# Attention in 64 units on one Trainium2 core: the copy of the attended values waits for earlier outputs, and the softmax's last sum and minimum become one operation per head

## What is computed

```python
x = rmsnorm(hidden_states, ln_weight)
h_q, h_k, h_v = x @ w_q.T, ctx @ w_k.T, ctx @ w_v.T          # 32 heads of 128
score = einsum('bqhd,bkhd->bhqk', h_q, h_k) + position_bias
score = where(mask, score, -inf)
attn = einsum('bhqk,bkhd->bqhd', where(mask, softmax(score), 0), h_v)
out = hidden_states + attn @ w_out.T
```

## Time and profile before

| what | value |
|---|---|
| three runs | 1131.38, 1131.36, 1126.65 us; median 1131.36 |
| the profiled execution | 1131.8 us, its span 1130.0 us |
| mean granted clock of PE in the span | 0.939 |
| busy: PE, DVE, POOL, ACT | 1042.1, 810.8, 552.7, 516.4 us |
| attention loop | some 372 to 979 us, 37.6 us for one pair of heads |

### The profile page before, as it was taken

The page is one execution under the profiler, slowest core; times in us unless marked ns, Lnnn a source line. Parts: engine busy times, 40 slices in busy tenths (PEclk is TensorE's granted clock), DMA queues, the critical chain, the costliest instruction groups (busy, mean ns, idle before and its releaser), DMA issues.

```text
span 1130.0 us, 18045 instructions
## 1 busy us (share of the span) xinstructions
PE 1042.1 (92%) x5664; PEld 902.2 (80%) x5664; DVE 810.8 (72%) x1389; ACT 516.4 (46%) x1279; POOL 552.7 (49%) x507
## 2 busy tenths in 40 slices
PE   8999999999999779888988898889888988899995
PEld 7887888999999668777877787778777877677874
DVE  6778676665655788777977797779777977854525
ACT  6744454322222545545554555455545555245251
POOL 0356665544532665454645564556555555324113
PEclk9999999999999898889988998899889988799998
DMA  7534444544442623122312231223222312110010
GB/s 253 179 127 160 159 163 173 179 157 169 150 159 94 218 75 117 60 79 93 116 60 79 93 116 61 81 90 116 63 80 89 116 42 94 51 53 1 1 38 37
DMA packets 57585, 119.81 MB, mean 106 GB/s; under 512 B 7232, under 2 KB 11328, under 8 KB 57536
## 3 DMA queue, kind: packets, MB, share of 16 engines
q1 hardware_dynamic: 57536, 119.19, 31.2%
HBM read 83.51 MB, written 35.65 MB: 105 GB/s over the span
## 4 chain that ended last, share of the span: by engine, by line
PE 69%; DVE 4%; issue 4%; ACT 3%; POOL 1%; ACTq 0%; POOLq 0%; DVEq 0%
PE psum L1772 18%; PE psum L1773 18%; PE psum L1774 18%; PE psum L1778 9%; PE psum L1779 3%; PE psum L1934 2%; DVE pt L1336 1%; ACT av_hi L924 1%; ACT mix L924 1%; ACT pt L924 1%; POOL stat L865 0%; PE psum L2029 0%; DVE rsum L1682 0%; POOL mix L694 0%; POOL stat L867 0%
## 5 line engine op out<-in xcount | busy, mean ns | idle before, releaser
L694 POOL TENSOR_TENSOR mix<-kf,mix 128x512 fp32r<-128x512 f32 x64 | 82.2, 1284 | 262.7 <-ACT mix L924 262.6
L1772 PE MATMUL psum<-mix,av_hi 128*128 128x256 f32 (+1 forms) x512 | 180.8, 353 | 3.4 <-POOL mix L694 1.9
L1778 PE MATMUL psum<-pt,av_hi 128*128 128x256 f32 x256 | 77.3, 378 | 61.6 <-DVE pt L1336 60.4
L924 ACT ACTIVATE av_hi<-psum 128x512 fp32r<-128x512 f32 x76 | 45.1, 594 | 172.1 <-PE psum L1774 126.7
L1778 PEld LDWEIGHTS psum<-pt,av_hi 128*128 128x128 f32 x256 | 57.0, 223 | 70.9 <-DVE pt L1336 67.6
L1772 PE MATMUL psum<-xn_lo,ext_hi 128*128 128x512 f32 x256 | 112.8, 441 | 0.0
L1772 PEld LDWEIGHTS psum<-mix,av_hi 128*128 128x128 f32 x512 | 98.7, 193 | 12.1 <-POOL mix L694 2.1
L1773 PE MATMUL psum<-xn_hi,ext_lo 128*128 128x512 f32 x256 | 106.8, 417 | 0.0
L1774 PE MATMUL psum<-xn_hi,ext_hi 128*128 128x512 f32 x256 | 104.9, 410 | 0.0
L1774 PE MATMUL psum<-mix,av_hi 128*128 128x512 f32 x256 | 102.5, 400 | 0.0
L1773 PE MATMUL psum<-mix,av_lo 128*128 128x512 f32 x256 | 102.0, 399 | 0.0
(11 more groups left out here) (251 smaller groups left out, 3235.4 us busy)
## 6 DMA issues: line engine op xcount, KB each, us to landing
kf<-k_blocks SPq DMA_DIRECT2D x64, 256.0 KB, 2.7
wvq_hi<-v_blocks SPq DMA_DIRECT2D x64, 256.0 KB, 2.8
raw<-in_wk SPq DMA_DIRECT2D x16, 512.0 KB, 3.6
k_blocks<-far SPq DMA_DIRECT2D x32, 256.0 KB, 2.2
raw<-in_wv SPq DMA_DIRECT2D x16, 512.0 KB, 4.3
v_blocks<-rows SPq DMA_DIRECT2D x32, 256.0 KB, 2.2
raw<-in_wq SPq DMA_DIRECT2D x16, 512.0 KB, 3.2
raw<-in_wo SPq DMA_DIRECT2D x16, 512.0 KB, 3.3
```

The costliest lines, as they stand in the source:

```text
L694: g.tensor_tensor(dst_lo, src, dst_hi, ALU.subtract).then_inc(s_lo, 1)
L924: return a.activation(dst, src, ACT.Copy)
L1772: mm(out, lhs(0), rhs(1), start=first, stop=False)
L1778: mm(out, lhs(0), rhs_both, start=True, stop=False)
```

## The change

Three things change together.

First, in attended_hi for j = 0 the count is 8g - 8 in the place of 8g - 4. The others keep theirs.

Second, the scores carry the opposite sign: the norm weights `lnw` are multiplied by -1 once on POOL, `far` holds +2^100 for a masked key, the bias is subtracted, and the exponential is taken with scale -1. The maximum becomes a minimum, clamped by starting at 2^99. Each head's last sum and its minimum are one call, tensor_tensor_reduce, which DVE carries out as two instructions. The semaphore scores_full counts four a unit, and its users' counts are multiplied by four.

Third, attended is cut in two: `rest` (attended_rest) stands between the first sum and the minimum operations.

```diff
@@ gpsimd
+                    g.tensor_scalar(lnw[:, :], lnw[:, :], -1.0, None, ALU.mult).then_inc(s_lnw_negated, 1)
+                    pool.wait_ge(s_lnw_negated, 1)
                 g.tensor_tensor(rows[:, tile % 2], rows[:, tile % 2], lnw[:, :], ALU.mult).then_inc(s_xn_ready, 1)
...
-                nc.gpsimd.tensor_tensor(bm, far[:, HB * hf:HB * hf + HB, :], g_, ALU.add).then_inc(s_bm_ready, 1)
+                nc.gpsimd.tensor_tensor(bm, far[:, HB * hf:HB * hf + HB, :], g_, ALU.subtract).then_inc(s_bm_ready, 1)
@@ scalar
-                act.wait_ge(s_max_neg, n + 1)
+                act.wait_ge(s_scores_full, 4 * n + 4)
...
-                    a.activation(soft[parity][:, b, :], soft[parity][:, b, :], ACT.Exp, bias=nmax[:, 1, b:b + 1],
+                    a.activation(soft[parity][:, b, :], soft[parity][:, b, :], ACT.Exp, bias=nmin[:, b:b + 1], scale=-1.0,
...
-                        attended_hi(n - 1, 8 * g - 4 + (4 if j == 3 else -4 if j == 0 else 0) + (0 if j else 4), prev(j))
+                        attended_hi(n - 1, 8 * g - 4 + (4 if j == 3 else -4 if j == 0 else 0), prev(j))
@@ vector, softmax_in
                 v.tensor_tensor(s, psS[:, :, 0], bm, ALU.add).then_inc(s_scores_sum, 1)
                 dve.wait_ge(s_scores_sum, n + 1)
-                v.tensor_tensor(s, psS[:, :, 1], s, ALU.add).then_inc(s_scores_full, 1)
-                dve.wait_ge(s_scores_full, n + 1)
-                v.tensor_reduce(nmax[:, 0, :], s, AX.X, ALU.max).then_inc(s_scores_max, 1)
-                dve.wait_ge(s_scores_max, n + 1)
-                v.tensor_scalar(nmax[:, 1, :], nmax[:, 0, :], -0.5 * FAR, -1.0, ALU.max, ALU.mult
-                                ).then_inc(s_max_neg, 1)
+
+            def softmax_min(n, parity):
+
+                s = soft[parity]
+                for b in range(HB):
+                    v.tensor_tensor_reduce(s[:, b, :], psS[:, b, 1], s[:, b, :], 1.0, 0.5 * FAR, ALU.add, ALU.min,
+                                           nmin[:, b:b + 1]).then_inc(s_scores_full, 1)
...
-            def attended(n, j):
+            def attended_rest(n, j):
 
                 dve.wait_ge(s_a_hi, n + 1)
                 v.tensor_tensor(rest[:, :, :], psA[:, :, 0], heads_out(0, j), ALU.subtract).then_inc(s_a_rest, 1)
+
+            def attended(n, j):
+
                 dve.wait_ge(s_a_rest, n + 1)
                 v.tensor_tensor(heads_out(1, j), psA[:, :, 1], rest[:, :, :], ALU.add).then_inc(s_a_lo, 1)
@@ vector, pair_dve
                     softmax_in(n + 1, (j + 1) % 2)
+                    if not (is_first(g) and j == 0):
+                        attended_rest(n - 1, prev(j))
+                    softmax_min(n + 1, (j + 1) % 2)
@@ tensor, scores
-                    pe.wait_ge(s_scores_full, n)
+                    pe.wait_ge(s_scores_full, 4 * n)
```

More of the change, by code:

```diff
@@ L119, in build @@
         prep = sb("prep", [P, 7, B])
-        nmax = sb("nmax", [P, 2, HB])
+        nmin = sb("nmin", [P, HB])
         esum = sb("esum", [P, 3, HB])
@@ L225, in build @@
         s_scores_full = sem("scores_full")
-        s_scores_max = sem("scores_max")
-        s_max_neg = sem("max_neg")
+        s_lnw_negated = sem("lnw_negated")
         s_exp_done = sem("exp_done")
@@ L1504, in group_dve @@
                     dve.wait_ge(s_kst[C12], 16 * PAIRS)
-                    v.tensor_scalar(far[:, :, :], m8[:, :, :], -1.0, FAR, ALU.add, ALU.mult).then_inc(s_far_ready, 1)
+                    v.tensor_scalar(far[:, :, :], m8[:, :, :], -1.0, -FAR, ALU.add, ALU.mult).then_inc(s_far_ready, 1)
                 dve.wait_ge(s_xc, q + 1)
@@ L1600, in _ @@
             softmax_in(0, 0)
+            softmax_min(0, 0)
             lo_of(s_q_hi, s_q_lo, 2, qk[1][:, 0], banks[5], qk[0][:, 0])
@@ L1630, in pair_dve @@
                     if last and j == 3:
+                        attended_rest(n - 1, j - 1)
                         attended(n - 1, j - 1)
@@ L1641, in pair_dve @@
                         y_stats(2)
+                        attended_rest(n, j)
                         attended(n, j)
@@ L1959, in outputs @@
                         pe.wait_ge(s_q_lo, units)
-                        pe.wait_ge(s_scores_full, units)
+                        pe.wait_ge(s_scores_full, 4 * units)
                         pe.wait_ge(s_o_add, 2 * (o - 2) + i + 1)
```

## The result

The changed kernel takes 1032.1 us (median of four runs, 1031.9 to 1033.0) against 1131.4 us (1126.7 to 1131.9). The ratio is 0.913, with a 95% interval of 0.911 to 0.916. The forecast was 1034.6 us.

What follows compares the result with a forecast made beforehand. PE was taken as the bound, stalled 15 times by a wait in attended_hi. 1131.8 - 94.7 (stalls) - 2.5 (first pair) = 1034.6 us, between 1028 and 1041; the range with rival 1 was 1027 to 1056.

Steps and rivals of the forecast that it cites:

- What bounds the kernel: Attention loop: PE is the bound; 15 stalls of 6.31 us come from attended_hi's wait for outputs in j = 0.
- The term: Attention loop, j = 0: asking for 8g - 8 outputs removes all 15 stalls of 6.31 us, 94.7 us.
- What is late next: Unit j = 0 with the new order: no stall takes the old one's place while m is below 2.9 us.
- The chain in j = 0: DVE operations from the scores' first sum to the probabilities' low part: done at 680.1 + m, PE wants them at 682.98.
- m, the new operations: DVE time for a unit's four sum-and-minimum pairs: 1.6 us, between 1.1 and 2.4.
- The sign given: Profile after, DVE: the new pair of instructions should show at about 0.4 us per head.
- The point at which DVE decides: Steady loop: DVE instead of PE sets the unit's time from m = 2.2 us on.
- The rival itself: DVE becomes the bound in the loop: at m = 2.4, 20 us more, 1055 us; chance 0.13.
- DVE's half gives PE nothing in the loop: Steady loop: DVE's unit falls from 7.80 to 7.2 us beside PE's 7.81, giving only room of 0.6 us.
- First and last pair: Ends of the loop: first pair gains 2.5 us, of 0 to 6; last pair 0, within 1.5.
- The extra pass on POOL: Sign of the norm weights, once, near 110 us: costs 0, at most 1.5 us if the transposes were late.
- The clock: Granted clock of 1.00 through the loop; rival that it does not hold: 0.95, 30 us, 1065 us, chance 0.04.

Runs made afterwards that it cites:

- the last experiment: Three kernels on one chip: changed kernel 1032.9 us, the new wait alone 1035.3 us, changed kernel with another POOL order ahead of the loop 1031.7 us.
- four sets: Changed kernel with the four sum-and-minimum pairs of each unit done four times on DVE, extra outputs unused: 1113.8 us.
- that kernel: Changed kernel with attended_hi in j = 0 asking for 8g - 5 outputs instead of 8g - 8: 1090.0 us, ratio 0.966.

## Why the prediction was right, step by step

- **What bounds the kernel.** Right. Each stall was idle time and a slow unit after it, both by the one number in attended_hi; the wait alone took all 15 away. The term was 94.7 us and measured 96.2, because the stalls cost 6.4 us on average and the pair whose rows were priced 6.31. Part of the good fit of the total is luck: the sum starts from an execution of 1131.8 us, at the top of what the kernel before showed. On the chip of the last experiment its median is 1126.2 us, and the whole change gains 93.3 us where 97.2 were forecast.
- **What is late next.** Right: nothing. The chain in j = 0 was to end at 680.1 + m against 682.98; with the 0.85 us measured it would have 2 us to spare. The trace has 1.18 us, from the end of the low part at 603.33 to attend at 604.51, since DVE waited 0.90 us for ACT's copy of the probabilities just before it. The prediction's chain went through DVE alone and left that copy out. With the wait alone, where DVE is the later one, 0.55 to 0.70 us are left.
- **m, the new operations.** Mis-sized. The prediction took 1.6 us with ends at 1.1 and 2.4; it is 0.85, below the low end. The step that failed is the read: it was given 0.09 to 0.19 us of its own, by ACT's reads, and costs nothing, as it lies inside the next operation. The sign given, 0.4 us per head, measured 0.21. It had no effect, since the operations lie beside PE's work.
- **The point at which DVE decides.** m = 2.2 was given, 2.5 measured. The prediction's unit of DVE without m (7.2 - 1.6 = 5.6 us) is 0.3 us longer than the one measured at four sets: 6.16 - 0.85 = 5.3. The rival itself was sound, and the four-set run shows its price.
- **DVE's half gives PE nothing in the loop.** Right: 1.000 with the old wait, and 2.5 us with the new one, outside the steady loop.
- **First and last pair.** 2.5 us for the first and 0 for the last; the loop's first three units gave 1.1, the last two 0.8. Together with the beginning and the feed-forward stage it is 3.4 us against 2.5, within what single executions differ by.
- **The extra pass on POOL.** Taken as 0, at most 1.5 us. It is a small cost: it delays the start of the loop by 0.7 us. It took 1.51 us and PE waited for the product behind it:

```profile
L715 POOL TENSOR_SCALAR lnw<-lnw x1: 1508/1508/1508, 110.3 to 110.3; 128x512 f32<-128x512 f32 x1
```

```profile
114.45 0.66 PE L1843 MATMUL psum<-ident,rows 128*128 128x128 f32 x4 [0.43 <-POOL rows L717]
```

  POOL's first operation of the loop starts at 370.2 to 370.7 us in the nine profiles with the pass and at 369.6 to 369.8 in the three without; counted from POOL's first operation with the norm weights it is 260.34 to 260.36 us against 259.67 in all of them. How much of that reaches the end of the kernel was not measured apart. The prediction argued from a PE that was busy in that stretch; it asked what PE did there, and not who waits for POOL's next product.
- **The clock.** Right that it holds: 1.00 in 423 us of unbroken work.

## What to carry to other kernels

A small idle time that recurs with the same length once per round of a loop can be a wait with one number in it, as here: find the instruction that ends it and ask whose work that count protects. Price such a stall with the slow unit behind it, which here was four tenths of the whole. Work taken from DVE, busy for 72%, was worth nothing in the steady loop, since its unit was not longer than PE's; so measure the room (here by adding work until the time moves) before shortening it.

## What was unexpected

The granted clock after a pause of about 2.35 us fell in 8 of 15 cases and stayed at 1.00 in 7, with identical work around it, in an order that repeats every four pairs; the runs of that kernel lie between 1086.2 and 1092.1 us, so a kernel with such pauses is not judged by one execution. And a DVE operation of 0.69 us can take 2.94 when a POOL operation starts 0.02 us ahead of it. Added work in front of it brought the two together six times in the four-set kernel's loop; the changed kernel has no such case there between 400 and 860 us.
